# Scatter sums of a graph network as two fp16 passes with an exact 0/1 mask, and turns, edge windows and waits moved around them

## The reference

```python
h = relu(layernorm(x)); x = x + GAT2(relu(GAT1(h)))      # layers 1 and 2
h = relu(layernorm(x)); x = x + GCN2(relu(GCN1(h)))      # layers 3 and 4
# GAT: h = x @ W; softmax over each node's edges of leaky_relu(a_s[src] + a_d[dst]);
#      out = segment_sum(alpha * h[src], dst) + b
# GCN: h = x @ W; out = segment_sum(h[src] * dinv[src] * dinv[dst], dst) + b
```

## Time and profile before

| | before |
|---|---|
| median of 3 runs | 2168.01 us (2162.92 to 2172.12) |
| the profiled execution | 2162.72 us, span of its engines 2160.5 us |
| busy: PE, DVE, ACT, POOL | 97%, 66%, 44%, 39% of the span |
| mean granted TensorE clock | 0.991 |
| DMA | 451.94 MB, mean 209 GB/s |

### The profile page before, as it was taken

One profiled execution on the slowest core, in us unless ns is written; L12 is line 12 of the kernel. 1 busy time (PEld: TensorE's weight loads), 2 busy tenths in 40 slices (PEclk: granted clock), 3 DMA queues, 4 the chain that ended last, 5 costly groups with the idle time before them and its releaser, 6 DMA issues.

```text
span 2160.5 us, 34890 instructions
## 1 busy us (share of the span) xinstructions
PE 2103.2 (97%) x12917; PEld 1312.5 (61%) x12917; DVE 1418.8 (66%) x3186; ACT 951.1 (44%) x1328; POOL 851.6 (39%) x1067
## 2 busy tenths in 40 slices
PE   7999999999999999999998999999998999999997
PEld 4666666556666666666665556666665666656664
DVE  8989754435776675435897888565466547876652
ACT  4444454434554554444554454333333343334442
POOL 3221167614332321344544443443344422336552
PEclk9999999999999999999999999999999999999999
DMA  5998899994555559998786443576797626776552
GB/s 185 237 223 200 229 216 195 214 233 161 192 176 196 197 180 245 230 219 217 261 282 214 166 161 132 165 248 223 265 318 281 226 103 213 245 223 215 196 193 93
DMA packets 297486, 451.94 MB, mean 209 GB/s; under 512 B 193267, under 2 KB 193465, under 8 KB 297190
## 3 DMA queue, kind: packets, MB, share of 16 engines
q1 hardware_dynamic: 256950, 277.12, 46.0%
q0 software_dynamic: 40368, 172.60, 25.5%
HBM read 234.94 MB, written 179.89 MB: 192 GB/s over the span
## 4 chain that ended last, share of the span: by engine, by line
PE 86%; DVE 6%; DMA 3%; ACT 2%; issue 2%; POOL 1%; SPq 0%; POOLq 0%; ACTq 0%; DVEq 0%
PE ps_h L1077 67%; PE ps_h L1096 9%; PE ps_z L1040 4%; PE ps_e L1175 1%; PE ps_e L1176 1%; PE ps_e L1165 1%; PE ps_e L1166 1%; DMA rows<-e_out 1%; DVE edge_mem L1393 1%; DVE bn L1264 1%; DVE x_keep L1290 0%; DVE x_keep L1286 0%; DMA edge_mem<-meta_rows 0%; DMA out<-res,perm_out 0%; DVE res L1382 0%
## 5 line engine op out<-in xcount | busy, mean ns | idle before, releaser
L1077 PE MATMUL ps_h<-w_hi,x_keep 128*128 128x384 f16 x2568 | 526.4, 326 | 1.1 <-issue 1.1
L1077 PE MATMUL ps_h<-w_hi,z_hi 128*128 128x384 f16 x1572 | 388.0, 329 | 1.5 <-DVE w_lo L1254 1.5
L1077 PE MATMUL ps_h<-w_lo,z_hi 128*128 128x384 f16 x1572 | 387.4, 328 | 0.0
L1077 PE MATMUL ps_h<-w_hi,z_lo 128*128 128x384 f16 x1572 | 386.4, 328 | 0.0
L1077 PEld LDWEIGHTS ps_h<-w_hi,x_keep 128*128 128x128 f16 x2568 | 249.9, 98 | 164.7 <-issue 2.4
L1077 PE MATMUL ps_h<-w_lo,x_keep 128*128 128x384 f16 x1284 | 313.7, 326 | 0.0
L903 ACT ACTIVATE row_out<-ps_h,grow 128x768 f32<-128x768 f32 x159 | 142.9, 899 | 366.8 <-PE ps_h L1077 365.9
L1330 DVE TENSOR_TENSOR z_lo<-ps_z,z_hi 128x768 f16<-128x768 f32 x131 | 125.0, 954 | 155.5 <-ACT z_hi L916 155.4
L734 POOL TENSOR_SCALAR veps<-mv 128x1 f32<-128x1 f32 x158 | 43.8, 277 | 458.0 <-DVE mv L1267 455.5
L1361 DVE TENSOR_TENSOR res<-z,res 128x768 f16<-128x768 f32 x107 | 102.3, 956 | 183.7 <-ACT res L949 94.3
L1077 PEld LDWEIGHTS ps_h<-w_lo,z_hi 128*128 128x128 f16 x1572 | 154.9, 99 | 104.1 <-issue 3.6
(11 more groups left out here) (252 smaller groups left out, 3609.9 us busy)
## 6 DMA issues: line engine op xcount, KB each, us to landing
rows<-row_out SPq DMA_DIRECT2D x199, 384.0 KB, 3.8
rows<-e_out SPq DMA_DIRECT2D x60, 384.0 KB, 4.6
row_in<-in_x SPq DMA_DIRECT2D x40, 384.0 KB, 4.3
row_in<-rows SPq DMA_DIRECT2D x40, 384.0 KB, 5.1
x_rows<-pre SPq DMA_DIRECT2D x40, 384.0 KB, 3.7
res<-x_rows SPq DMA_DIRECT2D x40, 384.0 KB, 4.4
pure_rows<-row_out SPq DMA_DIRECT2D x39, 384.0 KB, 2.6
row_in<-pure_rows SPq DMA_DIRECT2D x39, 384.0 KB, 4.9
```

Source lines behind the costliest of these rows:

```text
L1077: last = nc.tensor.matmul(ps_h[s][:, a, 0:HALF], zp[:, c, :], wp[:, c, a * HALF:(a + 1) * HALF], start=(c == 0 and zp is zh and wp is hi), ...
```

## The change

Each sum of layers 3 and 4 becomes two fp16 passes. The mask is copied to fp16 once (`same_parts` on ACT, four pieces, and `same_rows` on DVE, which scales the carry row). ACT scales the gathered rows by a power of two into an upper fp16 part (`sum_parts`, after the carry), DVE makes the lower part (`low_sums`), and `sum_mm` adds both passes in PSUM; `edge_sums` and `last_result` scale back. The scale of layer 4 comes from a running maximum (`sum_top`, `spread_top`, `fourth_scale`). The sums of layer 3 go to the two buffers of `last_out`, each with its own semaphore (`plain_store`). `put_batch` turns the tiles of a batch that follows other tiles three windows apart. `EDGES[2]` and `plain_at` start one window later, and ACT does `weights` and `sum_carry` before `make_z`. `sum_mm` waits for both parts and for `same_half`, no longer for the carry itself.

```diff
-        follows = b > 0 and seq[g - 1].chain
-        last = [t.g for t in seq if t.chain and t.layer == 4][-THREE:]
-        turns = [last[0], last[1], g - 1] if last and b > 0 and last[1] >= g - 12 else [g - 3, g - 2, g - 1]
+        apart = 1 if seq[g - 1].chain else 3
+        turns = [g - 1 - 2 * apart, g - 1 - apart, g - 1]
...
-    EDGES = {1: begin["2"] + 2, 2: begin["3"] + 2}
-    plain_at = {begin["4"] + 4 + (7 * j) // 5: j for j in range(ET)}
+    EDGES = {1: begin["2"] + 2, 2: begin["3"] + 3}
+    plain_at = {begin["4"] + 5 + (7 * j) // 5: j for j in range(ET)}
...
+            def plain_store(j):
+                sp.wait_ge(edge_done, 2 * ET + j + 3)
+                sp.dma_start(table_tile(3, NT + j), last_out[j % 2]).then_inc(plain_stored[j % 2], 16)
...
                 for t in turned[:1]:
                     upper_parts(t)
+                if gat and not first and now is not None:
+                    weights(now + h0)
+                if w in plain_at:
+                    sum_carry(3, plain_at[w])
+                if w in last_at:
+                    sum_carry(4, last_at[w])
+                k = w - EDGES[2] - 2 * ET
+                if 0 < k <= 4:
+                    same_parts(k - 1)
                 for t in due(w + 1):
                     make_z(t)
...
             def sum_carry(layer, j):
...
+                last.then_inc(carry_ready, 1)
+                act.wait_ge(carry_ready, j + (layer - 1) * ET + 1)
+                if h >= 2:
+                    act.wait_ge(e_summed, 2 * ET + h - 1)
+                nc.scalar.activation(sum_parts[h % 2][:, 0, :], to, ACT.Copy, scale=sum_by[layer]).then_inc(sum_hi_ready, 1)
+
+            def same_parts(k):
+                n = ET // 4
+                act.wait_ge(mask_ready, ET)
+                act.wait_ge(negmax_ready, 2 * ET)
+                nc.scalar.activation(same_half[:, k * n:(k + 1) * n, :], same_t[:, k * n:(k + 1) * n, :], ACT.Copy).then_inc(same_ready, 1)
...
             def sum_mm(layer, j):
...
+                pe.wait_ge(same_ready, 5)
+                pe.wait_ge(sum_hi_ready, h + 1)
+                pe.wait_ge(sum_lo_ready, h + 1)
+                pe.wait_ge(edge_done, j + (layer - 1) * ET + 2)
+                for k in range(2):
+                    nc.tensor.matmul(e_lo, same_half[:, j, :], parts[:, k, 0:SPLIT], start=k == 0, stop=k == 1, skip_group_check=True)
+                    last = nc.tensor.matmul(ps_e[:, 1, 0:D - SPLIT], same_half[:, j, :], parts[:, k, SPLIT:D], start=k == 0, stop=k == 1,
+                                            skip_group_check=True)
+                last.then_inc(e_summed, 1)
...
+                if t.layer == 4:
+                    n = t.pos - PURE
+                    dve.wait_ge(sum_top_step, n + 1)
+                    V.tensor_tensor(sum_top[(n + 1) % 2], sum_top[n % 2], top[s4][:, :], ALU.max).then_inc(sum_top_step, 1)
...
+            def low_sums(layer, j):
+                h, rows = j + (layer - 3) * ET, last_src[j % 4]
+                parts = sum_parts[h % 2]
+                dve.wait_ge(sum_hi_ready, h + 1)
+                V.scalar_tensor_tensor(parts[:, 1, :], rows, sum_by[layer], parts[:, 0, :], ALU.mult, ALU.subtract).then_inc(sum_lo_ready, 1)
+                if layer == 4:
+                    dve.wait_ge(last_in[j % 4], (ET // 4 + j // 4 + 1) * 32)
+                    base = last_base[j % 4]
+                    V.tensor_tensor(base[:, D:D + 1], base[:, D:D + 1], sum_down[4], ALU.mult).then_inc(sum_base_ready, 1)
...
+                if w in plain_at:
+                    low_sums(3, plain_at[w])
+                if w in last_at:
+                    low_sums(4, last_at[w])
                 for t in due(w + 2):
                     (prepare_first if t.layer == 1 else prepare_third if t.layer == 3 else prepare_even)(t)
```

More of the change, by code:

```diff
@@ L69 @@
 THREE = 3
+CARRY = 2.0 ** -12
 def order_of_tiles(NT, PURE, FREE, batches):
@@ L398, in build @@
         z3_hi = row_iota[:, 11 * P:11 * P + KC * THREE * P // 2].bitcast(F16).rearrange("p (c q) -> p c q", c=KC)
+        far_flat = rank_mem[:, 0, :]
+        sum_parts = [far_flat[:, 0:D].bitcast(F16).rearrange("p (a n) -> p a n", a=2), e_prod.bitcast(F16).rearrange("p (a n) -> p a n", a=2)]
+        same_half = far_flat[:, D:D + ET * P // 2].bitcast(F16).rearrange("p (t q) -> p t q", q=P)
+        sum_sc = sb("sum_sc", [P, 10])
+        sum_top = [sum_sc[:, k:k + 1] for k in range(2)]
+        sum_down, sum_by = ({3: sum_sc[:, 4 + k:5 + k], 4: sum_sc[:, 6 + k:7 + k]} for k in range(2))
         e_diag, e_arg, e_wt, e_wt_t = (row_iota[:, (k + 1) * P:(k + 2) * P] for k in range(4))
@@ L501, in build @@
         e_stored = sem("e_stored")
+        same_ready = sem("same_ready")
+        sum_scaled = sem("sum_scaled")
+        sum_top_step = sem("sum_top_step")
+        sum_spread = sem("sum_spread")
+        sum_spread_all = sem("sum_spread_all")
+        sum_hi_ready = sem("sum_hi_ready")
+        sum_lo_ready = sem("sum_lo_ready")
+        sum_base_ready = sem("sum_base_ready")
+        plain_stored = [sem(f"plain_stored{s}") for s in range(2)]
         base_stored = [sem(f"base_stored{s}") for s in range(3)]
@@ L743, in load @@
                     if t.mixed and t.pos == FREE:
-                        pool.wait_ge(e_stored, 16 * ((t.layer - 1) * ET + 1))
+                        if t.layer == 4:
+                            for s in range(2):
+                                pool.wait_ge(plain_stored[s], (ET + 1 - s) // 2 * 16)
+                        else:
+                            pool.wait_ge(e_stored, 16 * ((t.layer - 1) * ET + 1))
                     rows_free(pool, t)
@@ L974, in window @@
                     divide(before + h0)
[L975 to L980, removed]
                 for t in turned[1:]:
@@ L1007, in sum_carry @@
             def sum_carry(layer, j):
-                to = last_src[j % 4]
+                to, h = last_src[j % 4], j + (layer - 3) * ET
+                act.wait_ge(sum_scaled, layer - 2)
                 act.wait_ge(last_in[j % 4], ((layer - 3) * (ET // 4) + j // 4 + 1) * 32)
@@ L1169, in sum_mm, with spread_top @@
             def sum_mm(layer, j):
[L1170 to L1177, removed]
+                h = j + (layer - 3) * ET
+                parts = sum_parts[h % 2]
[8 more added lines that the diff above has]
+                last.then_inc(e_summed, 1)
+            def spread_top():
+                pe.wait_ge(sum_spread, 1)
+                nc.tensor.matmul(e_small, ones[:, :], e_diag[:, :], start=True, stop=True, skip_group_check=True).then_inc(sum_spread_all, 1)
             def all_max(layer):
@@ L1430, in edge_sums @@
                 else:
-                    dve.wait_ge(e_stored, (h + 1) * 16)
-                    base = last_base[j % 4]
-                    V.tensor_tensor(e_out[:, 0:SPLIT], base[:, 0:SPLIT], e_lo, ALU.add)
-                    V.tensor_tensor(e_out[:, SPLIT:D], base[:, SPLIT:D], ps_e[:, 1, 0:D - SPLIT], ALU.add).then_inc(edge_done, 1)
+                    if j < 2:
+                        dve.wait_ge(e_stored, (2 * ET + 1) * 16)
+                    else:
+                        dve.wait_ge(plain_stored[j % 2], (j // 2) * 16)
@@ new lines, in same_rows, with sum_scale, third_scale @@
+            def same_rows():
+                dve.wait_ge(same_ready, 4)
+                V.tensor_scalar(same_half[0:1, :, :], same_half[0:1, :, :], 1.0 / CARRY, None, ALU.mult).then_inc(same_ready, 1)
+            def sum_scale(layer, by_top):
+                step(V.tensor_copy(sum_by[layer], by_top))
+                V.memset(sum_by[layer][0:1, :], CARRY).then_inc(sum_scaled, 1)
+            def third_scale():
+                step(V.tensor_copy(sum_down[3], chain_sc[:, 2:3]))
+                sum_scale(3, chain_sc[:, 3:4])
@@ new lines, in top_to_spread, with fourth_scale @@
+            def top_to_spread():
+                dve.wait_ge(sum_top_step, NT - PURE + 1)
+                V.tensor_scalar(e_diag[:, :], ident[:, :], sum_top[(NT - PURE) % 2], None, ALU.mult).then_inc(sum_spread, 1)
+            def fourth_scale():
+                dve.wait_ge(sum_spread_all, 1)
+                sc = sum_sc
+                step(V.tensor_reduce(sc[:, 2:3], e_small, AX_X, ALU.max))
+                step(V.tensor_scalar(sc[:, 2:3], sc[:, 2:3], w_scale[:, 3, 1:2], float(D), ALU.mult, ALU.mult))
+                step(V.tensor_scalar(sc[:, 2:3], sc[:, 2:3], TINY, None, ALU.max))
+                down = sum_down[4]
+                step(V.tensor_scalar(down.bitcast(I32), sc[:, 2:3].bitcast(I32), EXPONENT, None, ALU.bitwise_and))
+                step(V.tensor_scalar(down, down, 2.0 ** -14, None, ALU.mult))
+                step(V.reciprocal(sc[:, 3:4], down))
+                sum_scale(4, sc[:, 3:4])
@@ L1711, in _ @@
                     chain_scales()
+                if w == begin["3m"]:
+                    third_scale()
+                    same_rows()
+                if w == begin["5"] - 3:
```

(3 more changed lines are left out.)

24 lines of the change are left out of this document (15 added, 9 removed).

## The result

The changed kernel takes 2171.32 us (median of 12 runs, 2166.55 to 2178.03), the kernel before 2167.38 (12 runs, 2162.92 to 2172.12): ratio 1.0022, interval 1.0011 to 1.0032. It is 3.9 us slower, inside the forecast range and inside half a per cent; the forecast had 3 us faster. The profiled execution of the changed kernel took 2169.43 us, span 2167.4, 6.9 us longer than the span of before.

What follows compares the result with a forecast made beforehand. TensorE, busy 97% of the span, was taken to bound the kernel. The terms -25.6 + 18.4 - 12.3 - 1.4 + 2.6 - 2.7 + 18 gave -3.0 us: 2165 against the median 2168.0, range 2134 to 2194.

Steps and rivals of the forecast that it cites:

- passes: 40 sums on TensorE: four fp16 matmuls take 0.65 us instead of 1.29, giving back 25.6 us.
- waits for `low_sums`: TensorE before the 40 sums: waits for DVE's lower part, 0.45 us where nothing waited before, together 18.4 us more.
- two buffers: Stores of layer 3's sums: waits of 2.5 and 7.60 us and 2.2 us of clock go, 12.3 us less.
- four batches: Batches under the second GAT, shifted one window: 13 us longer, plus 1.3 us of clock per batch, 18 us more.
- GAT start: Second GAT's beginning: its gather has one window more before the first dots, about 2.7 us less.
- turns before 178: Turns set apart before batch 178: DVE has no slack, more work precedes `low_parts` in window 171, 2.6 us more.
- turns in 4m: Turns set apart in 4m: 3.7 us against 3.35 and 1.7 of clock before, 1.4 us less.
- Rival (a): Second GAT's shift is harmless and weights ahead of `z` take away 9.9 us: 2137 us, chance 0.25.
- Rival (b): DVE's lower parts come late at most sums, mean wait 1.0 instead of 0.46: +21.6, 2187 us, chance 0.15.
- Rival (d): Sum passes as dear as fp32 if weight loads set the pace: +25.6, 2191 us, chance 0.04.
- (c): Clock falls at both waits of each GAT batch and in 170 and 172: +7 and +5, 2177 us, chance 0.10.
- Rival (e): Clock swings at every one of the 40 sums, losing 1.7 us each: +68, 2233 us, chance 0.03.

Runs made afterwards that it cites:

- e7: The kernel before with only the sums of layer 3 in the two buffers of `last_out` and their stores as in the change: 2160.03 us (0.9952).
- e6: The changed kernel without the sums' lower parts; the second pass multiplies zeros and nothing waits for `low_sums`: 2151.79 us (0.9912).
- e1: The changed kernel with the second GAT's edge windows back at 160: 2158.14 us (0.9966).
- e2: The changed kernel with the second GAT's edge windows one window later still, from 162: 2153.05 us (0.9944).
- e12: The changed kernel run once more, unchanged: 2173.83 us (1.0031).
- e5: The changed kernel with each sum's matmuls after the window's 36 matmuls instead of after 24; a second turned tile's `low_parts` precedes sums on DVE: 2152.48 us (0.9920).
- e3: The changed kernel with ACT's weights again behind `z`, the carry and the division; the sums' carry stays ahead of `z`: 2167.16 us (1.0004).
- e8: The changed kernel with edge windows from 162 and the sums after the window's 36 matmuls: 2135.63 us (0.9852).
- e10: The changed kernel with edge windows from 162, sums after the window's 36 matmuls, and ACT's weights behind `z`: 2127.72 us (0.9820).

## Why the prediction was right or wrong

The terms against what the runs showed:

| term | forecast | measured |
|---|---|---|
| passes | -25.6 | -25.8: 20 sums of layer 4 without waits, 209.58 (e7) to 196.69 (e6), 0.64 each, taken for all 40 |
| waits for `low_sums` | +18.4 | +22.2 (changed kernel against e6) |
| two buffers | -12.3 | -11.1 in the profile, -9.9 in the medians (e7) |
| four batches | +18 | +16.3; back at 44.0 each in e1 and e2 |
| GAT start -2.7, turns before 178 +2.6 | -0.1 | +5.0, and +5.4 in e12; +1.7 and +3.3 in e5 and e6 |
| turns in 4m | -1.4 | -1.3, and +1.4 in e12 |
| layer 1, not in the sum | 0 | +2.2 |

The measured column adds up to 7.5 us; the two spans differ by 6.9. The medians are 3.9 apart, since the profiled execution of before lay 4.7 us under its median and that of the changed kernel 1.9 under its own.

**Right.** The mechanism of the large terms, with place and size: sums of 0.65 us; waits of 0.2 to 0.6 before most of them, released by `low_sums`; the stores' waits gone; batches of 46.7 to 48.4 us (47 to 49 forecast) with gaps at the end of S3 and P2 and a wait for `z` behind each. The gaps were smaller than added up (0.76 for 1.3, 1.98 for 2.4). Rival (a) falls with these batches, and with e3: putting the weights ahead takes none of the 9.9 us away (in the four batches TensorE waits 15.5 us for the weights and `z` with the weights ahead, 16.0 in e3). Rival (b) needed a mean wait of 0.8; it was 22.2 / 40 = 0.56. Rival (d) falls with the 0.65 us. Of (c) three of the eight pairs of waits in the four batches brought a lower clock, all at the end of P2, which is what the 1.3 us per batch had paid for; it also fell at the waits in 171 and 172, for 6.8 us, but over windows 158 to 177 it was at half only 3.4 us longer than before.

**Wrong, the sign.** Forecast -3.0, measured +6.9 in the profile and +3.9 in the medians. Two steps failed. First, "about 0.1 more for the signal and weights not loaded ahead": it measured 0.26, and 0.16 more (0.26 - 0.1) at each of 37 sums is 6 us; the waits came out 3.8 larger, with smaller errors the other way. What of the 0.26 is the signal and what the weight load stays open. Second, the terms for windows 158 to 177.

"Its gather has one window more before the first dots: about -2.7" failed. In the kernel before, DVE waited for that gather and TensorE then 2.36 us for the weights; the 2.75 us that sized the term stand twelve windows later, in 173:

```profile
1036.70 0.96 DVE L1393 CUSTOM_DVE_ANT_0 edge_mem<-edge_mem,atts_bc 128x768 f32<-128x768 f32 x1 [2.68 <-DMA edge_mem<-rows,pos_dst]
...
1047.43 0.33 PE L1158 MATMUL ps_e<-ident,rank_mem 128*128 128x128 f32 x1 [2.36 <-ACT e_self L996]
...
1139.88 0.33 PE L1158 MATMUL ps_e<-ident,rank_mem 128*128 128x128 f32 x1 [2.75 <-ACT e_self L996]
```

In the changed kernel the gather is in time, but DVE stands about as long in the same window (160) for another transfer, the rows `row_x` of the tile that it prepares:

```profile
1039.51 0.96 DVE L1330 TENSOR_TENSOR pre<-row_in,row_x 128x768 f32<-128x768 f32 x1 [3.25 <-DMA row_x<-in_x,perm_x]
```

So it is in e2, e3, e5, e6 and e12 (3.25 to 3.78 us), while e1, with the edge windows back at 160, waits for the gather again (2.22). TensorE's waits for the weights went from 2.36 + 2.75 = 5.11 us to 1.26 + 2.24 with 0.59 for `z` behind each, 4.68: 0.4 us and not 2.7. ACT's new order is not the reason: with it undone (e3) they are 5.57.

The turns cost more than the net 2.6 us that I had. The first turn of window 172 waited 4.92 us for the batch tile's `low_parts` (4.92 in e12 too, 2.96 and 3.24 in e5 and e6):

```profile
1118.55 0.33 PE L1195 MATMUL ps_e<-ident,rank_mem 128*128 128x128 f32 x1 [2.24 <-ACT e_self L1019]
1119.47 0.87 PE L1075 MATMUL ps_z<-ident,z 128*128 128x128 f32 x6 [0.59 <-ACT z L957]
1133.06 1.51 PE L1075 MATMUL ps_z<-ident,z 128*128 128x128 f32 x6 [4.92 <-DVE z_lo L1374]
```

All waits of turns for `low_parts` in these windows are 8.25 us against 3.96, so +4.3 (+2.3 and +2.6 in e5 and e6). The rest is mostly the clock, at half for 13.7 us against 10.2, 1.7 us for which I had no term.

With ACT's order undone (e3) the 5 us are gone, but as clock: the idle time stays, 12.7 us for 13.0. That one order brings a lower clock and the other does not is seen in four profiled executions with the weights ahead (13.7, 13.7, 10.2 and 10.2 us at half) against one with them behind `z` (3.4); with the edge windows from 162 it is 6.8 us either way (e8, e10). How much of the clock's part is the order, and how much chance, stays open.

**Rival (e)** was named after the page "TensorE: Matmul & The Clock Gate" of the Trainium skill, section "A second HAM failure mode: psum-queue depth-cycling", which tells of a kernel whose clock swung because TensorE idled briefly between groups of matmuls again and again. In the sums here the trace does not show that. The stretch view of the changed kernel, windows 228 to 247 and 286 to 315:

```profile
1543.45:1689.33 145.88, 140.09 (x892) 88.27 (x890) 110.16 (x213) 69.63 (x95) 64.61 (x59) 1.00 0.87 312
1945.80:2153.28 207.48, 199.91 (x1234) 120.26 (x1231) 134.29 (x225) 103.32 (x158) 114.03 (x121) 1.00 0.57 186
```

31 sums, waits before nearly all, and the granted clock is 1.00. After the first 23 us of this execution it fell in six places: near a wait of 4.92 us, and near pairs of waits close together (1.26 and 0.59, 1.14 and 2.19, and at the end of P2 in three batches 1.9 to 2.0 and 0.59); in the fourth batch the same pair left it at 1.00.

## What to carry to other kernels

Splitting a matmul for speed adds a producer for each part: count when the last part is ready against where the matmul stands in its engine's order, and move the matmul rather than the producer if there is room behind it. Here the passes brought 26 us, the wait for the second part took 22 back, and putting the sum behind the window's products returned all of it. Before counting on a wait to go, ask what its engine would wait for next: here the gather was given a window more, and the engine stood as long for another transfer. When a repeating schedule is shifted against another with a period of its own, add up the windows for both phases: one window's shift cost 16 us, two windows' 2.5.

## What the runs showed of the hardware

The first matmul of a sum started 0.26 us after the record of `low_sums` ended, in 39 of 40 sums of the changed kernel (0.30 in the other), and the list of waits shows 0.16 us less than TensorE lost. The same work in the same order ran 161.3 to 165.1 us in windows 158 to 177 (four executions of three kernels, two of them of one: 164.6 and 165.1), with the clock at half for 10.2 to 13.7 us: a difference of a few us between two kernels in such a stretch does not show what their edits did. In windows 40 to 78 two executions of one and the same kernel lay 4.1 us apart.
